# A GpSimd gather program in a graph layer: from a hardware loop with copied index lists to written-out code on the source table

## What is computed

```python
# N = 6250 nodes, E = 200000 edges sorted by dst, 16 relations, 8 bases
feat  = layernorm(x)
w_rel = einsum('rb,bdo->rdo', w_comp, weight)
msg   = einsum('nd,rdo->rno', feat, w_rel)[etypes, src] * edge_weight
x     = x + relu(segment_sum(msg, dst) + h_bias + feat @ loop_weight)
# experts: 16, two per node, 256 -> 512 -> 256, on layernorm(x)
x     = x + layernorm(h + moe(h)) * gamma + beta       # h = layernorm(x)
```

## Time and profile before

| | |
|---|---|
| median of 3 runs | 2809.38 us (2808.56 to 2809.4) |
| the profiled execution | 2809.64 us, its span 2807.4 us |
| TensorE busy, mean granted clock | 2223.8 us (79%), 0.912 |
| GpSimd busy | 1810.5 us (64%) |
| VectorE, ScalarE busy | 965.7 us, 653.3 us |
| DMA | 339.11 MB, 121 GB/s on average |
| first and last gather of the graph layer start at | 165.21 us, 2162.84 us |

### The profile page before, as it was taken

The page is one execution under the profiler, slowest core; times in us unless marked ns, Lnnn a source line. Parts: engine busy times, 40 slices in busy tenths (PEclk is TensorE's granted clock), DMA queues, the critical chain, the costliest instruction groups (busy, mean ns, idle before and its releaser), DMA issues. The chain is left out here.

```text
span 2807.4 us, 44573 instructions
## 1 busy us (share of the span) xinstructions
PE 2223.8 (79%) x11549; PEld 1851.5 (66%) x11550; DVE 965.7 (34%) x2172; ACT 653.3 (23%) x1539; POOL 1810.5 (64%) x2000
## 2 busy tenths in 40 slices
PE   1779999999998888786776767567556579999987
PEld 0568787877777666665564646446444379999975
DVE  6743333242243322221321212112112543333347
ACT  2532323233222212111111010001000233233245
POOL 0557767777777777777777777777776035555544
PEclk9999999999999989998898878778877799999998
DMA  6544434444443434334333333333333642222246
GB/s 207 168 146 120 131 108 123 122 118 142 116 122 114 136 109 119 115 115 129 108 109 116 119 112 103 108 100 116 105 103 90 225 152 69 69 71 69 71 134 219
DMA packets 146325, 339.11 MB, mean 121 GB/s; under 512 B 36674, under 2 KB 56290, under 8 KB 146051
## 3 DMA queue, kind: packets, MB, share of 16 engines
q0 software_dynamic: 89296, 245.33, 29.9%
q1 hardware_dynamic: 39311, 59.54, 6.2%
q10 hardware_dynamic: 17588, 32.88, 3.6%
HBM read 292.84 MB, written 47.97 MB: 121 GB/s over the span
## 5 line engine op out<-in xcount | busy, mean ns | idle before, releaser
L1069 POOL DMA_INDIRECT rows<-feat,idx x1540 | 1464.3, 951 | 492.0 <-issue 432.2
L1278 PE MATMUL psW<-rows,S 128*128 x3920 | 1065.6, 434 | 379.0 <-SPq L1026 347.0
L1278 PEld LDWEIGHTS psW<-rows,S 128*128 128x128 f32 x3920 | 843.6, 220 | 596.7 <-issue 460.0
L1150 DVE TENSOR_TENSOR S<-psHere,coefS 128x896 f32<-128x896 f32 x280 | 301.2, 1090 | 1346.5 <-PE psW L1278 1338.4
L1338 ACT COPY z<-psW 128x512 f32<-128x512 f32 x196 | 114.7, 585 | 1427.4 <-PE psW L1278 1426.7
L1244 PE MATMUL psG<-wb,zT 128*128 128x256 f32 (+1 forms) x1600 | 353.5, 379 | 0.0
L1244 PEld LDWEIGHTS psG<-wb,zT 128*128 128x128 f32 (+1 forms) x1600 | 301.1, 188 | 44.2
L1729 PE MATMUL psH<-xT,w1x 128*128 128x128 f32 x1840 | 226.8, 277 | 0.2
L1680 POOL DMA_INDIRECT expert_rows<-os,at_rows x114 | 113.7, 997 | 171.8 <-DVE os L1788 171.8
L1729 PEld LDWEIGHTS psH<-xT,w1x 128*128 128x128 f32 x1840 | 216.4, 193 | 2.0 <-issue 1.9
L1738 PE MATMUL psO<-w2s,hT 128*128 x912 | 215.8, 380 | 0.0
(11 more groups left out here) (284 smaller groups left out, 1439.7 us busy)
## 6 DMA issues: line engine op xcount, KB each, us to landing
rows<-feat,idx POOLq DMA_INDIRECT x1568
g<-expert_rows SPq DMA_DIRECT2D x24, 512.0 KB, 5.1
w1s<-in_L_ffn_w SPq DMA_DIRECT2D x8, 1024.0 KB, 10.0
w2s<-in_L_ffn_w SPq DMA_DIRECT2D x16, 512.0 KB, 10.1
feat<-rows SPq DMA_DIRECT2D x24, 256.0 KB, 3.0
fts<-feat ACTq DMA_DIRECT2D x24, 256.0 KB, 2.9
h<-in_x ACTq DMA_DIRECT2D x24, 256.0 KB
y_rows<-y ACTq DMA_DIRECT2D x24, 256.0 KB
```

The lines of the kernel that those rows point to most:

```text
L1069: e.indirect_dma_start(rows[:, at * H:(at + 1) * H], None, d.feat, bass.IndirectOffsetOnAxis(ap=idx[:, q * GB + u:q * GB + u + 1], axis=0) ...
L1150: e.tensor_tensor(S[h0 + h][:, :].rearrange("p (s b n) -> p s b n", s=U, b=B), both[:, h * U:(h + 1) * U, :].unsqueeze(2).to_broadcast([P, ...
L1278: last = e.matmul(psW[:, bass.ds(bank[u], H)], S[h][:, u * ZC:(u + 1) * ZC], rows[:, bass.ds(slot[u], H)], start=False, stop=True, skip_gr ...
```

## The change

GpSimd's program of the graph layer becomes straight code. The 110 groups from block 28 on are written out, each wait is for a constant (or, for the ring, for one of eight registers, loaded once for eight groups as before). The lists `idx` and the copies into them go, in the stage ahead too; the indirect DMA takes its index column from `srcT` itself. The increments `s_paced` and `s_turn` of the paced waits go, except the one behind the ring's wait. Nothing changes on the other engines.

```diff
@@ expand, GpSimd @@
-                e.indirect_dma_start(rows[:, j * H:(j + 1) * H], None, d.feat, bass.IndirectOffsetOnAxis(ap=idx[:, j:j + 1], axis=0)).then_inc(s_row[j % ROWS], 16)
+                e.indirect_dma_start(rows[:, j * H:(j + 1) * H], None, d.feat, bass.IndirectOffsetOnAxis(ap=srcT[:, j:j + 1], axis=0)).then_inc(s_row[j % ROWS], 16)
...
-                    for q in range(EG + 1):
-                        e.tensor_copy(idx[:, q * GB:(q + 1) * GB], srcT[:, q * GB:(q + 1) * GB]).then_inc(s_list, 1)
                     e.wait_ge(s_feat, 16 * NT2)
-                    e.wait_ge(s_list, EG + 1)
@@ graph_layer, GpSimd @@
-            ch = Chain(e, s_pool)
             regs, room_held = ([e.alloc_register(f"{n}{q}") for q in range(IB)] for n in ("room", "room_held"))
-            last = NBLK // (IB * GB) - 1
-
-            def list_in(group, q):
-                ch.add(e.tensor_copy(idx[:, q * GB:(q + 1) * GB], srcT[:, bass.ds(group * GB, GB)]))
-
-            def landed(i, n):
-
-                e.wait_ge(s_in, i * (IB * GB) + (n + 1))
-                e.sem_inc(s_paced, 1)
-
-            def blocks(i):
-                e.load(regs, room[0:1, bass.ds(i * IB, IB)])
-                free = at_least_one(e, regs, room_held)
-                for q in range(0 if later(i) else EG, IB):
-                    if later(i) or q >= RB // GB:
-
-                        e.wait_ge(s_P, free[q])
-                        e.sem_inc(s_turn, 1)
-                    if later(i) or q > EG:
-                        ch.wait()
-                    if q < IB - 1 or not isinstance(i, int) or i < last:
-                        list_in(i * IB + q + 1, (q + 1) % IB)
-                    else:
-                        e.sem_inc(s_turn, 1)
-                    for u in range(GB):
-                        at = (q * GB + u) % RB
-                        landed(i, q * GB + u - AHEAD)
-                        e.indirect_dma_start(rows[:, at * H:(at + 1) * H], None, d.feat, bass.IndirectOffsetOnAxis(ap=idx[:, q * GB + u:q * GB + u + 1], axis=0)).then_inc(s_row[at % ROWS], 16)
...
-            blocks(0)
-            with e.Fori(1, last) as i:
-                ch.base, ch.n = IB * i - EG, 0
-                blocks(i)
-            ch.base, ch.n = IB * last - EG, 0
-            blocks(last)
+
+            def blocks(group):
+
+                if group % IB == 0 or group == EG:
+                    i = group // IB
+                    e.load(regs, room[0:1, i * IB:(i + 1) * IB])
+                    at_least_one(e, regs, room_held)
+                if group >= RB // GB:
+                    e.wait_ge(s_P, room_held[group % IB])
+                    e.sem_inc(s_turn, 1)
+                for j in range(group * GB, (group + 1) * GB):
+                    e.wait_ge(s_in, j - AHEAD + 1)
+                    e.indirect_dma_start(rows[:, j % RB * H:(j % RB + 1) * H], None, d.feat, bass.IndirectOffsetOnAxis(ap=srcT[:, j:j + 1], axis=0)).then_inc(s_row[j % ROWS], 16)
+            for group in range(EG, NBLK // GB):
+                blocks(group)
@@ gnn @@
-        idx = sb("idx", [P, IB * GB], I32)
```

More of the change, by code:

```diff
@@ L647, in _, with expand @@
                 src_columns(q)
-def expand(nc, d, wcd, halfs, win_n, ident, tables, wend, pairs, jcol, wcol, spread, dstS, wgtS, coefS, s_got, s_feat, srcT, idx, rows, s_row):
+def expand(nc, d, wcd, halfs, win_n, ident, tables, wend, pairs, jcol, wcol, spread, dstS, wgtS, coefS, s_got, s_feat, srcT, rows, s_row):
     from contextlib import ExitStack
@@ L699, in expand @@
         s_js, s_cz, s_ctl = sem("js"), sem("ctl_ready"), sem("ctl")
-        s_near, s_list = sem("near_st"), sem("lists")
+        s_near = sem("near_st")
         s_lst = [sem(f"late_st{k}") for k in range(DL)]
@@ L965, in _, with graph_layer @@
             e.tensor_scalar(ident[:, :], ident_i[:, :], 0.0, None, ALU.is_equal)
-def graph_layer(nc, d, a, ctl, pairs, room, wend, srcT, dstS, wgtS, coefS, ident, wb, lw, hb, gw, s_w, logit, choice, mean, rstd, idx, rows, s_row):
+def graph_layer(nc, d, a, ctl, pairs, room, wend, srcT, dstS, wgtS, coefS, ident, wb, lw, hb, gw, s_w, logit, choice, mean, rstd, rows, s_row):
     from contextlib import ExitStack
@@ L1002, in graph_layer @@
         s_in = sem("rows_in")
-        s_pool, s_turn, s_paced, s_zr, s_node = sem("pool"), sem("pool_turn"), sem("pool_paced"), sem("zero"), sem("node")
+        s_turn, s_zr, s_node = sem("pool_turn"), sem("zero"), sem("node")
         s_late = [sem(f"late{k}") for k in range(len(CHUNK))]
@@ L2013, in gnn @@
             coefS = sb("coefS", [P, NEAR * CS * B])
-            expand(nc, d, wcd, halfs, win_n, ident, tables, wend, pairs, jcol, wcol, spread, dstS, wgtS, coefS, got, s_feat, srcT, idx, rows, s_row)
+            expand(nc, d, wcd, halfs, win_n, ident, tables, wend, pairs, jcol, wcol, spread, dstS, wgtS, coefS, got, s_feat, srcT, rows, s_row)
         wb, lw, hb, gw = sb("wb", [P, HC, B, H]), sb("lw", [P, HC, H]), sb("hb", [P, H]), sb("gw", [P, HC, X])
-        graph_layer(nc, d, a, ctl, pairs, room, wend, srcT, dstS, wgtS, coefS, ident, wb, lw, hb, gw, s_w, logit, choice, mean, rstd, idx, rows, s_row)
+        graph_layer(nc, d, a, ctl, pairs, room, wend, srcT, dstS, wgtS, coefS, ident, wb, lw, hb, gw, s_w, logit, choice, mean, rstd, rows, s_row)
 def program(nc, a, out):
```

## The result

The changed kernel takes 2764.91 us (median of 4 runs, 2761.35 to 2769.09) against 2808.97 us for the kernel before on the same chip: ratio 0.9844, 95% interval 0.9827 to 0.9861. That is 44 us faster. The profiled execution took 2769.09 us (span 2767.1), 40.5 us less than the one of before.

What follows compares the result with a forecast made beforehand. The prediction took GpSimd's gathers to pace the graph layer after about 460 us, TensorE before. Jumps 3.5 + 14.5 and lists 6 made 24.0 us off 2809.6, giving 2785.6 us, range 2779 to 2798.

Steps and rivals of the forecast that it cites:

- Registers, the extra increment, the 0.30 us gap: Graph-layer gathers on GpSimd: dropping each gather's register addition and separate increment gains nothing; the 0.30 us idle stays.
- The holes every 106 gathers: GpSimd, graph layer: small holes of about 1.4 us, one at 732.02, pass across loop turns and stay unchanged.
- Jumps back: GpSimd's graph-layer loop: all 11 holes of 2.15 us at taken jumps go, worth 3.5 + 14.5 us.
- the six jumps: Later loop jumps not beside a SyncE slice: 22.4 us across less 7.9 usual, 14.5 us gained, low end 13.3.
- TensorE's limit at block 448: At 717 us TensorE's turn freeing ring blocks caps earlier jump and list gains at 3.5 us, ends 0 and 4.9.
- the two jumps behind SyncE's slices: Jumps at 1299 and 1589 us, hidden behind SyncE's absence: worth nothing, as GpSimd then meets the longer wait.
- The 4.75 us distance: One of six later jumps, measured across between gathers; may hold 1.2 us of something else, hence low end 13.3.
- Lists: GpSimd, graph layer: 79 groups after block 448 lose their list copy, gaining 6 us, range 5.2 to 7.1.
- The wide table: Gathers reading index columns from the wide source table: costs nothing; rival says 34 us more, 2820 us, chance 0.02.
- the straight code: Written-out graph-layer gathers on GpSimd: costs nothing; rival of partly priced code, 2801 to 2809 us, chance 0.11.
- TensorE paces longer: Rival, graph layer: TensorE is the bound until 900 us, so earlier gains don't count; 17.4 us gained, 2792, chance 0.10.
- The slower rivals: Written-out code starving GpSimd's queue, ending at 2824 us, chance 0.05; slow wide-table reads, 2820 us, chance 0.02.

Runs made afterwards that it cites:

- j_inc_behind: Changed kernel plus an increment of its own issued behind each gather, the wait staying on the gather: 2764.94 us against 2808.79 for the kernel before, ratio 0.9845.
- f_after: The changed kernel itself, timed again beside other runs on one chip: 2769.40 us against 2812.41 for the kernel before, ratio 0.9847.
- g_jumps: Changed kernel plus an always-taken branch over 640 unused increments at 11 places where the loop's passes began: 2775.42 us, ratio 0.9866 to the kernel before.
- g_lists: Changed kernel with only the index lists and their copies put back: 2775.86 us against 2813.12 for the kernel before, ratio 0.9867.
- f_inc: Changed kernel with a separate increment put back ahead of each gather, carrying the wait: 2782.90 us, ratio 0.9899 to the kernel before.
- g_inc_jumps: f_inc plus an always-taken branch over 640 unused increments at the 11 places where the loop's passes began: 2798.87 us, ratio 0.9946 to the kernel before.
- f_both: Kernel before with only the loop written out, copied lists and separate increments kept: 2790.89 us against 2812.41, ratio 0.9919.
- i_inc_behind: Changed kernel plus an increment issued behind each gather, wait on the gather, on a slow chip: ratio 0.9907 to the kernel before.

## Why the prediction was wrong in size

Step by step, by its own terms:

- **Registers, the extra increment, the 0.30 us gap: "I take nothing for it".** This is the step that failed. It is 13.5 us. I costed the increment as an instruction (right: nothing, j_inc_behind) and not as the place where the wait stands. I wrote that the wait "remains, on the gather itself" without asking where it had stood before.
- **The holes every 106 gathers, "so I leave them".** The same step seen from the other end. They were in the rows, and I kept them because nothing in the change touched them. Ten of them from gather 537 on hold 12.5 us more than ten usual distances, the size of the missing term. What the change touched was when the queue takes up a gather, and so whether the pause runs ahead of the count or behind it.
- **Jumps back, 3.5 + 14.5 = 18.0.** Measured 21.5 for the loop as a whole. In the two traces the six jumps that I had put at 14.5 gave 14.9. TensorE's limit at block 448 was read rightly: the traces differ by 7.0 us at the gather ahead of it and by 4.6 at it (717.16 and 712.53), and my bounds were 0 and 4.9. What was wrong is the two jumps behind SyncE's slices, which I valued at nothing: the gathers behind them gained 4.1 us, and with the slices' waits that follow 3.8 are left, about what the term was short. I had compared stretches from a slice with and without a jump and took the slice's wait as the master, and forecast waits of 2 to 3 us there once the jumps were gone; they are 1.28 and 0.81. At the other two slices the waits are shorter too, without any jump near (2.00 us instead of 3.00, 1.45 instead of 2.13), but these vary by up to 1 us between traces (1.26 and 0.96 in f_after, 1.93 and 1.95 in j_inc_behind), and what sets them was not tested. The 4.75 us distance, of which I suspected 1.2 us to be something else, was the jump behind a pause: g_jumps has 4.45 us there.
- **Lists, 6 us.** 5.8 to 6.5 alone (g_lists), 8.0 with the increments in place. Right, within the spread of the runs.
- **The wide table and the straight code, nothing.** Right: 951 ns per gather in both kernels, and no hole marked as issue over 0.4 us in the whole layer. (The code written out holds 1540 gathers, not the 1512 of my rivals; it changes nothing there.)
- **TensorE paces longer** (2792) did not come: what GpSimd gained reached the end, with 41.6 us at the last gather and 40.5 in the profiled execution's time. TensorE's waits for the count in 900 to 1000 us fell from 11.3 to 5.4 us, and between 2000 and 2100 from 43.8 to 40.7.
- **The slower rivals** did not come either; the densest starving of straight code that I had feared was one hole per 84 gathers, and there is none.

Together 13.5 + 3.5 + 2.0 = 19.0 us more than forecast, against 43.0 measured on that chip. The range failed with the sum, because an edit that I had costed at nothing had no upper end in it. The rule I had set for myself, to bound an unseen cost from both sides, I had applied to straight code and to the table, and not to the increment.

## What to carry to other kernels

On GpSimd ask of each wait which instruction carries it. Ahead of these gathers the queue stood still until the signal came in either case. But with the wait on the gather itself the queue had already taken the gather up, and its pause ran during the wait; with the wait on an increment ahead of it, the pause came after the signal, and 1.1 us of each showed. When equal holes stand at a regular spacing and nothing in the program explains them, look at what the engine's queue did there, and at which signal it had or had not yet got, before you call them fixed. Pair the queue's records with the engine's by counting, not by what stands nearest in time: by the nearest, I had the lead as 1 us where it was 2.2. And a jump on GpSimd has no price of its own: the same branch cost about 0.9 us or about 1.9 by what its queue was waiting on.

## What the runs showed of the hardware that I had not expected

- GpSimd's queue pauses for 3.1 us at every 106th gather of 128 rows: numbers 113, 219, 325 and on to 1491 in f_inc and g_inc_jumps (an increment per gather), in f_both (lists besides) and in before (a register addition besides, and the loop). It is there at all fourteen, hidden, in j_inc_behind too. The spacing stays 106 gathers with two instructions per gather (f_inc) and with three (before), so it goes by gathers and not by instructions; its cause is open.
- Instructions come to GpSimd in packets of 8.2 KB (0.77 MB in 94). The increment for each of 1540 gathers brought 12 packets (46 to 58), 64 bytes each, which cost no time.
- A load of eight registers takes about 564 ns on GpSimd's queue and starts 3.5 us before its group's first gather in the changed kernel (849.55 and 853.01), so it is not seen.
- Three of the chips ran all kernels a third slower, with TensorE's granted clock at 0.78 to 0.79 on average against 0.91 to 0.92. In i_inc_behind ScalarE's copies of the graph layer wait 1090 us in 60 waits for signals that the profile puts down to "remote", and TensorE's turns hold GpSimd up to 36.2 us at a time. Why is open. The change itself was not run on such a chip; the kernel with the increment behind the gather, which equals it on a chip of the usual speed, gained 0.8 and 0.9 per cent there.
